# Rotary rotation issued whole between two row maxima, additions behind it, and softmax row sums from four 32-column products instead of two of 64 columns

## What is computed

```
x = x + attn_a(layernorm(x))   # 16 heads of 64, q, k, v straight from x, softmax, output product
x = x + ffn(layernorm(x))      # 256 -> 1024 -> gelu -> 256
x = x + attn_b(layernorm(x))   # own layernorm, low-rank q, k, v (128), rotary turn of q and k, softmax, output product
x = x + ffn(layernorm(x))
```

## Time and profile before

| | |
|---|---|
| median of three executions | 3917.53 us (3916.56 to 3920.22) |
| the profiled execution, its own time | 3919.9 us |
| its span in the trace | 3918.1 us |
| mean granted TensorE clock | 0.974 of full |
| busy: PE, PEld | 3663.2 us (93%), 2362.5 us (60%) |
| busy: POOL, DVE, ACT | 2615.3 us (67%), 2277.8 us (58%), 1688.4 us (43%) |

### The profile page before, as it was taken

One profiled execution on the slowest core, in us unless ns is written; L12 is line 12 of the kernel. 1 busy time (PEld: TensorE's weight loads), 2 busy tenths in 40 slices (PEclk: granted clock), 3 DMA queues, 4 the chain that ended last, 5 costly groups with the idle time before them and its releaser, 6 DMA issues. The chain is left out here.

```text
span 3918.1 us, 60118 instructions
## 1 busy us (share of the span) xinstructions
PE 3663.2 (93%) x16736; PEld 2362.5 (60%) x16736; DVE 2277.8 (58%) x2988; ACT 1688.4 (43%) x3212; POOL 2615.3 (67%) x1467
## 2 busy tenths in 40 slices
PE   3999999999999999987874999999999999999799
PEld 2566666666666666646763565566555556555388
DVE  5444444444444444436665777777777777777343
ACT  1344444444444444434431444444444444444354
POOL 2677777878777877773222777787787777787511
PEclk9999999999999999998986999999999999999899
DMA  5333433343344333311014345544544554544100
GB/s 192 81 83 81 108 84 77 79 96 86 86 86 102 78 86 86 78 33 37 32 54 85 80 83 104 82 82 82 105 81 85 87 104 79 86 82 86 36 17 27
DMA packets 419600, 313.68 MB, mean 80 GB/s; under 512 B 254752, under 2 KB 292512, under 8 KB 418464
## 3 DMA queue, kind: packets, MB, share of 16 engines
q1 hardware_dynamic: 414400, 291.48, 37.5%
q10 hardware_dynamic: 5088, 20.97, 1.5%
HBM read 88.35 MB, written 21.50 MB: 28 GB/s over the span
## 5 line engine op out<-in xcount | busy, mean ns | idle before, releaser
L886 POOL TENSOR_TENSOR a_rs<-a_rs,a_p 128x1024 f32<-128x1024 f32 x384 | 916.0, 2386 | 318.6 <-ACT a_p L796 301.8
L886 POOL TENSOR_TENSOR b_rs<-b_rs,b_p 128x1024 f32<-128x1024 f32 x384 | 916.6, 2387 | 230.3 <-ACT b_p L796 212.0
L813 DVE TENSOR_REDUCE a_nmax<-a_ps_x 128x1 fp32r<-128x1024 f32 x512 | 627.2, 1225 | 758.8 <-PE a_ps_x L619 755.1
L813 DVE TENSOR_REDUCE b_nmax<-b_ps_x 128x1 fp32r<-128x1024 f32 x512 | 626.8, 1224 | 325.6 <-PE b_ps_x L619 321.6
L796 ACT ACTIVATE a_p<-a_ps_s 128x512 f32<-128x512 f32 x1024 | 529.5, 607 | 414.3 <-PE a_ps_s L635 414.1
L796 ACT ACTIVATE b_p<-b_ps_s 128x512 f32<-128x512 f32 x1024 | 530.4, 608 | 341.3 <-PE b_ps_s L635 336.3
L651 PE MATMUL b_ps_o<-b_p,b_v 128*64 128x512 f32 x2048 | 468.4, 599 | 0.0
L651 PE MATMUL a_ps_o<-a_p,a_v 128*64 128x512 f32 x2048 | 467.7, 598 | 0.0
L634 PE MATMUL b_ps_s<-b_q,b_k 128*128 128x512 f32 x1024 | 419.0, 409 | 9.1 <-DMA b_q<-b_nmax 6.3
L634 PE MATMUL a_ps_s<-a_q,a_k 128*128 128x512 f32 x1024 | 416.1, 406 | 1.7 <-DMA a_q<-a_nmax 1.6
L635 PE MATMUL b_ps_s<-b_q,b_k 128*128 128x512 f32 x1024 | 404.4, 395 | 0.0
(11 more groups left out here) (166 smaller groups left out, 5720.3 us busy)
## 6 DMA issues: line engine op xcount, KB each, us to landing
a_k<-a_nat_h SPq DMA_DIRECT2D x256, 128.0 KB, 2.4
a_q<-a_nat_h SPq DMA_DIRECT2D x256, 128.0 KB, 2.4
b_k<-b_nat_h SPq DMA_DIRECT2D x256, 128.0 KB, 3.9
b_q<-b_nat_h SPq DMA_DIRECT2D x256, 128.0 KB, 3.8
a_k<-a_nat_l SPq DMA_DIRECT2D x128, 128.0 KB, 2.4
a_q<-a_nat_l SPq DMA_DIRECT2D x128, 128.0 KB, 2.4
a_rinv<-rows_a SPq DMA_DIRECT2D x128, 128.0 KB, 2.9
b_k<-b_nat_l SPq DMA_DIRECT2D x128, 128.0 KB, 4.0
```

The lines of the kernel that those rows point to most:

```text
L813: dve.reduce_max(nmax[:, g % 2, head, qi:qi + 1], ps_x[:].rearrange("p a b -> p (a b)"), AX_X, negate=True).then_inc(s_red, 1)
L886: pool.tensor_tensor(out, out, p[:, bb, i, :], ALU.add).then_inc(s_sum, 1)
```

## The change

In `dve_window` the addition and the reciprocal move into a function `finish`. For attention b it is called behind the second `reduce` of the quarter, and both halves of the turn now stand between the two reduces. For attention a it is called where the additions stood, but the reciprocal now comes ahead of the addition. `row_sums` issues four products of 32 columns of weights over 256 queries each, in four column strips of the array, in place of two of 64 columns over 512 queries; ACT copies 256 columns in place of 512, and SP moves the sums with four DMAs of 64 lanes in place of two of 128.

```diff
-        ones = sb("ones", [P, D])
+        ones = sb("ones", [P, P // 4])
...
-        rb, rinv = sb("rb", [P, BLOCK]), sb("rinv", [P, BLOCK])
+        rb, rinv = sb("rb", [P, E]), sb("rinv", [P, BLOCK])
...
-            for head in range(2):
-                pe.matmul(ps_t[D * head:D * (head + 1), 1, :], ones[:], rs[:, g % 2, head * BLOCK:(head + 1) * BLOCK],
-                          start=True, stop=True).then_inc(s_r, 1)
+            for i in range(4):
+                pe.matmul(ps_t[32 * i:32 * (i + 1), 1, 0:E], ones[:], rs[:, g % 2, i * E:(i + 1) * E],
+                          start=True, stop=True, tile_position=(0, 32 * i)).then_inc(s_r, 1)
...
-                    act.activation(rb[:], ps_t[:, 1, :], ACT.Copy).then_inc(s_rb, 1)
+                    act.activation(rb[:], ps_t[:, 1, 0:E], ACT.Copy).then_inc(s_rb, 1)
...
-                if b in (0, 2) and live(t, 4, u - 3, NGROUP):
-                    add_out(dve, t, u - 3, b // 2)
-                if b == 0 and live(t, 4, u - 2, NGROUP):
-                    dve.wait_ge(s_rq, due(t, 128, 32 * (u - 1)))
-                    dve.wait_ge(s_row, due(t, 128, 32 * (u - 2)))
-                    dve.reciprocal(rqi[:], rq[:]).then_inc(s_recip, 1)
+                if rope is None:
+                    finish(dve, t, u, b)
                 if converting and rope is not None:
                     rotate_odd(dve, t, n)
+                    rotate_even(dve, t, n)
                 if live(t, 32, c + 1, 8 * NGROUP):
                     reduce(dve, t, c + 1)
-                if converting and rope is not None:
-                    rotate_even(dve, t, n)
+                if rope is not None:
+                    finish(dve, t, u, b)
                 if converting:
                     convert_lo(dve, t, n)
+
+        def finish(dve, t, u, b):
+
+            if b == 0 and live(t, 4, u - 2, NGROUP):
+                dve.wait_ge(s_rq, due(t, 256, 64 * (u - 1)))
+                dve.wait_ge(s_row, due(t, 128, 32 * (u - 2)))
+                dve.reciprocal(rqi[:], rq[:]).then_inc(s_recip, 1)
+            if b in (0, 2) and live(t, 4, u - 3, NGROUP):
+                add_out(dve, t, u - 3, b // 2)
...
-            sp.dma_start(rq[:, head, :], rb[D * head:D * head + 1, :].rearrange("o (p a) -> o p a", a=BT)
-                         ).then_inc(s_rq, 16)
+            for half in range(2):
+                row = D * head + 32 * half
+                sp.dma_start(rq[D * half:D * (half + 1), head, :],
+                             rb[row:row + 1, :].rearrange("o (p a) -> o p a", a=BT)).then_inc(s_rq, 16)
```

More of the change, by code:

```diff
@@ L777, in act_window @@
                 if b == 3 and live(t, 4, u - 1, NGROUP):
-                    act.wait_ge(s_r, due(t, 8, 2 * u))
-                    act.wait_ge(s_rq, due(t, 128, 32 * (u - 1)))
-                    act.activation(rb[:], ps_t[:, 1, :], ACT.Copy).then_inc(s_rb, 1)
+                    act.wait_ge(s_r, due(t, 16, 4 * u))
+                    act.wait_ge(s_rq, due(t, 256, 64 * (u - 1)))
+                    act.activation(rb[:], ps_t[:, 1, 0:E], ACT.Copy).then_inc(s_rb, 1)
                 if (u, b) == (0, 2) and live(t, 1, 0, BODIES):
@@ L880, in pool_window @@
                     if bb == 0:
-                        pool.wait_ge(s_r, due(t, 8, 2 * (w - 1)))
+                        pool.wait_ge(s_r, due(t, 16, 4 * (w - 1)))
                         pool.tensor_tensor(out, p[:, 0, 0, :], p[:, 0, 1, :], ALU.add).then_inc(s_sum, 1)
```

## The result

The changed kernel took 4261.68 us (median of five runs, 4260.94 to 4268.81) against 3920.22 us for the kernel before, run beside it: a ratio of 1.0877 (95% interval 1.0861 to 1.0893). The profiled execution has a span of 4259.9 us, 341.8 us over that of before. Its mean granted clock is 0.944, before 0.974.

The account below looks back on a forecast made before the run. PE, 93% busy, was taken to bound the kernel. Terms -31 + 226 + 107 + 18 - 6 + 9 = +323 us on 3919.9 gave 4243, less 2.4 for the median: 4241 us, range 4190 to 4330 (chance 0.65).

Parts of the forecast that it names:

- What bounds the kernel: PE, busy 93% of the span; `project_v` may start only when DVE's addition is done, 0.09 us before its load.
- The row sums, -31: In both attentions, four narrow products side by side save 0.27 us a place, less in b's windows 0 and 1: -31 us.
- The discount for windows 0 and 1: In b, row sums there wait about 0.1 us for quarter 2's addition, so 32 groups gain 0.17 us each.
- The stalls, +226: In b, `project_v` waits for the later addition: 29 times 3.8 us and 29 times 4.0 us, +226 us.
- The clock, +107: In b, PE's clock falls after each of 58 stalls, costing 1.85 us each: +107 us.
- the doubtful ones of 3.5 us: New PE idle times in b of 3.5 us, a little shorter than the shortest seen to bring the clock down.
- That 2.24 us left the clock up: One PE idle time of 2.24 us in b of the kernel before left the clock at 1.00.
- one by one: Rival case: the four row-sum products run singly, stream 1.7 us, total 4404 us; chance 0.05 together with only two side by side.
- SP, +18: In b's window 0, two extra DMA issues ahead of the stacks cost 1.2 us, 15 times: +18 us.
- faster rival: The addition ahead of `project_v` in b is not waited for: 3907 us, or 3889 with cheap DMA issues; chance 0.05.
- Window 1, -6: In b's window 1, PE's wait for quarter 1's first reduce goes away, 0.4 us 15 times: -6 us.
- Attention a, +9: In a's quarter 0, the reciprocal ahead of the addition delays `project_v` by 0.3 us, 29 times: +9 us.

Follow-up runs that it names:

- 3 to 5: Three variants of the changed kernel, attention b's addition behind the first reduce, half the turn or the whole turn: 3962.25, 4001.93 and 4155.11 us.
- sums_two: The kernel before with the four narrow products and short copy, its old order on DVE, and two DMAs for the sums: 3896.39 us, ratio 0.9937.
- fill: The changed kernel with twelve unused products ahead of the wait for the addition in attention b's `project_v`: 4160.83 us, ratio 1.0612.
- two_dmas: The changed kernel with the sums moved by two DMAs in place of four: 4237.58 us, ratio 1.0803.
- sums_only: The changed kernel with DVE's old order in both attentions, keeping narrow products, short copy and four DMAs: 3940.77 us, ratio 1.005.
- 8: The changed kernel with attention a's addition ahead of its reciprocal again: 4262.24 us, ratio 1.0870.
- add_after_even: The changed kernel with attention b's reciprocal and addition behind the whole turn, ahead of the second reduce: 4155.11 us, ratio 1.0595.
- order_only: The changed kernel with the row sums as before (two 64-column products, long copy, two DMAs), keeping the new DVE order: 4268.52 us, ratio 1.0886.
- one_dma: sums_two with one DMA for the sums, one for the reciprocals to DRAM, and the `nat_l` wait moved: 3874.86 us, ratio 0.9882.
- add_first: The changed kernel with attention b's reciprocal and addition directly behind the first reduce, ahead of the whole turn: 3962.25 us, ratio 1.0104.

## Why the prediction was right, point by point

- **What bounds the kernel.** Right: 0.09 us of slack ahead of `project_v` made the addition the thing to follow, and each step of it down DVE's list showed in the time (3 to 5).
- **The row sums, -31.** The price per place was 0.27; a's rows give about 0.3 and the periods of `sums_two` 0.26 to 0.29. The strips run side by side: eight records from 1079.44, the next at 1080.01. The discount for windows 0 and 1 was of the right kind, but too small: 28 times in b the load of L665 waits for L841, 1.03 us each, where in a it idles 0.81 us at the same place, so the addition costs some 0.2 us there, not 0.1.
- **The stalls, +226.** 58 waits. From the start of the maxima ahead of it to the start of L715 it is 4.33 to 4.43 us, before 0.46: 229 us lost in all (219.6 us is PE's idle time, which starts at the modelled end of a record). Part of the closeness is luck: from the first reduce to the turn it took 1.26 us and not 1.14, and from the reciprocal to the addition 0.10 and not 0.23, so quarters 0 and 2 lose nearly the same.
- **The clock, +107.** All 58 restarts are followed by a mean clock below 1.00 over 6 us, 0.67 on average; (1 - clock) x 6 adds up to 115 us. `fill` gave back 101 of them with the wait kept. PE's idle times came out at 3.70 to 3.81 us in both quarters, so the doubtful ones of 3.5 us did not arise. That 2.24 us left the clock up was thinner evidence than it looked: the same line of the kernel before idles once more in b, 2.43 us, and there the clock fell:

```profile
3231.09 0.79 PE L634 MATMUL b_ps_s<-b_q,b_k 128*128 128x512 f32 x1 [2.43 <-DMA b_q<-b_nmax]
...
3231.09:3237.09 6.00, 6.00 (x20) 3.65 (x22) 3.48 (x6) 2.40 (x4) 5.84 (x3) 0.73 0.49 98
```

- **SP, +18: right in b, with a share in a that it did not have.** In the changed kernel the removal of the two issues is worth 24 us. 19 of them (15 x 1.24) lie in the period from window 3 to 0, at the place foreseen: the second maxima of window 0's quarter 1 are loaded 15.80 us behind the last row sums, in `two_dmas` 14.56 (medians). Without the stalls it strikes both even windows and the changes of batch in a: with two DMAs the narrow products gain 24 us (`sums_two`), with four they lose 20 (`sums_only`). The prediction's faster rival (3907 us, or 3889) counted 18 us at most for it: had the addition not been waited for, the time would have been near 3941 us by `sums_only`, no gain at all. That rival itself was not run.
- **Window 1, -6: right.** PE's wait for quarter 1's first reduce is gone there: the second maxima of that quarter are loaded 13.88 us behind the last row sums, in `sums_only` 14.37 (medians), and quarter 2's first ones 0.38 us earlier than there. The row sums' wait for the addition then gives 0.2 us back.
- **Attention a, +9: too large.** PEld waits for the addition there 15 times, 6.0 us, and taking the reciprocal away changed nothing in the total (8); one period of four says 2 to 3 us. The three changes of batch, 27.4 to 28.2 us in place of 25.3, cost 8 us that the sum does not have.

In sum for b: 229 (stalls) + 115 (clock) + 21 (SP) - 9 (row sums in windows 2 and 3) - 5 (12 periods from window 0 to 1, 0.4 us each) = 351 us, against 346.3 measured.

The measured time is 21 us above the forecast. The two large terms were read from rows of the same kernel and were 3 and 8 us short. SP with its share in a was 6 us short, the row sums' wait for the addition some 3, and the kernel before ran 2.7 us slower this time; a's addition was 6 us too large.

Two things stay open. One is what, besides the idle time, decided whether the clock fell in `add_after_even`. The other is in attention a. Where a's changes of batch are longer, PE waits for the last `stack` DMA of q (9.2 us in `sums_only`, 8.0 in `sums_two`, 4.9 in the changed kernel; no such wait before, in `order_only` or in `one_dma`). That rules out the new order as the cause, but why that DMA is late in `sums_two`, which has as many DMAs as before, was not isolated, and from run to run the same code gives 27.4 to 30.9 us there.

## What to carry to other kernels

Before an operation is moved within an in-order engine's list, find who waits for it and with what slack: here 0.09 us, on an engine that was 93% busy, while the engine it moved on was 58% busy. A wait on TensorE is paid twice when it is long enough to bring the clock down, so short and long stalls are not in proportion (58 of 1.2 us cost no clock at all, 58 of 3.8 us cost 2.0 us more each). When a product is split into narrower ones, look at what carries its result: here the DMAs behind it were split too, and their issue on a shared queue cost more than the product saved. Merging them, with the two DMAs of the reciprocals, turned +0.5% into -1.2%. And an operation that waits for a DMA makes all behind it in its list wait: the reciprocal cost PE some 30 us when it stood one place earlier (`add_first`).

## What the runs showed of the hardware that I had not expected

- An idle time of 2.65 us on PE brought the clock down in 41 of 58 cases and left it up in 17, one of 1.2 us in none, one of 3.8 us in 58 of 58. Two idle times of 2.24 and 2.43 us at the same line in the kernel before went one each way. So the idle time alone does not decide it there.
- Four products of 32 columns with 256 rows each ran side by side: it is 0.57 us from their first record to the next load, where one by one was put at 1.7 us. The step from 64 to 32 columns cost about 0.1 us: from the start of the values to L665 it is 3.58 us in a, where L665 of the kernel before follows in the same form after 3.49.
- SP's issue of a DMA of the sums took 0.53 to 0.61 us (medians over all kernels) with 1, 2 or 4 KB alike, so here their number set their cost on the queue, not their size.
